# A four-stage graph network on one core: one-hots of the edge groups kept in DRAM, and the graph attention's work reordered

## What is computed

```python
h = relu(layernorm(x)); x = x + L0(h)     # weighted means over the edges, both directions
h = relu(layernorm(x)); x = x + L1(h)     # graph convolution, then 64 experts, top 2
h = relu(layernorm(x)); x = x + L2(h)     # 4 layers of attention by angle
h = relu(layernorm(x)); x = x + L3(h)     # 3 layers of graph attention, 4 heads

def _agnn_layer(h, src, dst, beta, n):    # L2, then relu
    h_norm = h * rsqrt(sum(h * h, -1, keepdims=True) + EPS)
    logits = beta * sum(h_norm[src] * h_norm[dst], -1)
    ex = exp(logits - segment_max(logits, dst, n)[dst])
    alpha = ex / (segment_sum(ex, dst, n)[dst] + EPS)
    return segment_sum(alpha[:, None] * h[src], dst, n)

def _gat_layer(x, src, dst, W, a_s, a_d, b):   # L3; every node below 1250 also has a loop
    h = (x @ W).reshape(n, 4, 64)
    e = leaky_relu(einsum(h, a_s)[src] + einsum(h, a_d)[dst], 0.2)
    ex = exp(e - segment_max(e, dst, n)[dst])
    alpha = ex / segment_sum(ex, dst, n)[dst]
    return segment_sum(h[src] * alpha[:, :, None], dst, n).reshape(n, 256) + b
```

## Time and profile before

| | |
|---|---|
| median of 3 runs | 11506.84 us (11502.91 to 11520.86) |
| span of the profiled execution | 10530.5 us, first to last instruction |
| the profiled execution's own time | not recorded apart; the median is 976.3 us above the span |
| mean granted TensorE clock | 0.835 of full speed |
| busy: PE, DVE, POOL, ACT | 6904.0, 5833.4, 5746.5, 2558.8 us |
| DMA | 825.78 MB, mean 78 GB/s |
| sort and first edge pass | up to about 220 us set-up, records to 1220 us, pass to 1957 us |
| attention by angle | 4472 to 7500 us |
| graph attention | 7612 to 10516 us |

### The profile page before, as it was taken

How to read it: one execution, slowest core, us unless ns; L and a number is a source line. 1 busy time by engine, 2 the same in 40 slices (tenths; PEclk the granted TensorE clock), 3 DMA queues, 4 the chain that set the end, 5 groups by cost and what they waited for, 6 DMA issues and landing times. The chain is left out here.

```text
span 10530.5 us, 156243 instructions
## 1 busy us (share of the span) xinstructions
PE 6904.0 (66%) x33524; PEld 5256.9 (50%) x33525; DVE 5833.4 (55%) x21353; ACT 2558.8 (24%) x6822; POOL 5746.5 (55%) x5970
## 2 busy tenths in 40 slices
PE   0000043333455579289799699699499989998997
PEld 0000033233244368178588588588356656665664
DVE  6000122322321311488788788788677768776887
ACT  0000000000000122122222222222155545554554
POOL 1777577676574021267477577477255535553553
PEclk9999999965676589699899899899767767777776
DMA  2000022424344079144544544544333333342333
GB/s 78 2 2 2 20 52 52 45 52 48 88 106 72 8 254 291 59 105 98 81 98 99 81 100 99 80 100 99 51 79 77 78 65 78 77 76 67 78 78 64
DMA packets 602104, 825.78 MB, mean 78 GB/s; under 512 B 297027, under 2 KB 423468, under 8 KB 602046
## 3 DMA queue, kind: packets, MB, share of 16 engines
q0 software_dynamic: 257472, 626.24, 29.4%
q1 hardware_dynamic: 344574, 198.99, 6.8%
HBM read 752.23 MB, written 72.83 MB: 78 GB/s over the span
## 5 line engine op out<-in xcount | busy, mean ns | idle before, releaser
L1258 POOL DMA_INDIRECT hs<-tab_agnn,rec x1984 | 1963.8, 990 | 1157.0 <-issue 594.3
L1692 POOL DMA_INDIRECT hs<-tab_gat,rec x1488 | 1406.6, 945 | 1294.5 <-DVE msg L1761 876.5
L511 PE MATMUL ps<-msg,oh 128*128 128x129 f32 x1984 | 510.5, 438 | 2040.8 <-DVE msg L486 2040.8
L511 PEld LDWEIGHTS ps<-msg,oh 128*128 128x128 f32 x1984 | 444.1, 329 | 2107.1 <-DVE oh L482 1229.3
L1868 PE MATMUL psV<-msg,ohf 128*128 128x260 f32 x2976 | 1279.6, 606 | 0.2 <-DVE msg L1761 0.2
L1730 DVE CUSTOM_DVE_ANT_0 cand<-psL,neg 128x512 f32<-128x512 f32 x1488 | 991.8, 686 | 258.0 <-issue 168.6
L1279 DVE CUSTOM_DVE_ANT_0 prod<-psG,hs 128x256 f32<-128x256 f32 x1984 | 841.9, 480 | 440.2 <-DMA hs<-tab_agnn,rec 359.9
L1868 PEld LDWEIGHTS psV<-msg,ohf 128*128 128x128 f32 x2976 | 902.1, 317 | 205.7 <-issue 1.5
L1408 PE MATMUL psV<-hs,pr 128*128 128x258 f32 x3968 | 998.2, 395 | 6.2 <-DVE pr L1318 6.2
L375 POOL DMA_INDIRECT rec_d<-slot x784 | 750.9, 958 | 425.3 <-DVE slot L356 235.0
L1384 PE MATMUL psG<-HN,ohT 128*128 x3968 | 969.7, 389 | 5.1 <-ACT neg L1353 5.1
(11 more groups left out here) (304 smaller groups left out, 12608.8 us busy)
## 6 DMA issues: line engine op xcount, KB each, us to landing
w<-in_L_gnn_w SPq DMA_DIRECT2D x224, 512.0 KB
hs<-tab_agnn,rec POOLq DMA_INDIRECT x1984
hs<-tab_gat,rec POOLq DMA_INDIRECT x1488
rec<-rec_d SPq DMA_DIRECT2D x1240, 8.0 KB
x<-xbuf SPq DMA_DIRECT2D x112, 128.0 KB, 4.1
ybuf<-y POOLq DMA_DIRECT2D x112, 128.0 KB, 4.3
tab_agnn<-H SPq DMA_DIRECT2D x4, 3250.0 KB, 11.4
xbuf<-acc SPq DMA_DIRECT2D x4, 3200.0 KB, 24.1
```

What stands on the lines that cost most here:

```text
L511: mm = nc.tensor.matmul(ps[:, j % 2, 0:cols], oh[:, j % 2, g, :], r, start=(g == 0), stop=(g == G - 1))
L1258: nc.gpsimd.indirect_dma_start(out=hs[:, j, g, :], out_offset=None, in_=k.tab_agnn, in_offset=bass.IndirectOffsetOnAxis(ap=rec[:, j, g, 0: ...
L1692: nc.gpsimd.indirect_dma_start(out=hs[:, j, g, :], out_offset=None, in_=k.tab_gat, in_offset=bass.IndirectOffsetOnAxis(ap=rec[:, j, g, 0:1 ...
```

## The change

1. The first edge pass (`sum_messages` with `keep=True`, key 0, by dst) keeps four buffers of one-hots, transposes each tile on PE, copies the transposes on ACT, and SP stores both to `oh_d` and `ohT_d` (124 x 128 x 512 float32 each). SP issues a group's stores four steps later and waits for all at the end.
2. Both attentions load them: `ohT` at lag 0, `oh` at lag 1, by SP. The making, transposing and copying of one-hots there goes.
3. Padding records point at row NP = 3200, and each table has 128 more rows, zeroed once; the two `below` minima go.
4. Graph attention: the two leaky steps become one over both parts, ACT copies `peak` and multiplies the messages of the fourth tile, DVE's message product (three tiles, one instruction) moves to the end of the step behind `acc`, and PE issues `psL` ahead of `psV`.
5. The semaphores of the two first stages are cleared and freed together, with a barrier.

```diff
 # sum_messages, keep
+        OR = U if keep else 2
+        oh = sb("oh", [P, OR, G, P], F32)
...
+                    if keep and (old := lagged(i, j, U)):
+                        _, _, t4 = old
+                        sp.dma_start(slab(k.oh_d, t4), oh[:, j, :, :].rearrange("p g e -> p (g e)")).then_inc(s_oh_kept[j], 16)
+                        sp.wait_ge(s_ohT, t4 + 1)
+                        sp.sem_inc(q.gate_sp, 1)
+                        sp.dma_start(slab(k.ohT_d, t4), ohT[:, j, :]).then_inc(s_ohT_kept[j], 16)
...
+                        for g in range(G):
+                            tr = nc.tensor.transpose(psT[:, j % 2, g * P:(g + 1) * P], oh[:, j, g, :], k.ident[:, :])
...
+                        nc.scalar.activation(ohT[:, j, :], psT[:, j % 2, :], ACT.Copy).then_inc(s_ohT, 1)
 # both attentions, SP (the angle's waits; graph attention waits q.v in place of s_p)
+                            if not (isinstance(i, int) and i == 0):
+                                sp.wait_ge(q.q, flow(t - U + 1))
+                            sp.dma_start(flat(ohT, j), slab(k.ohT_d, t)).then_inc(q.ld_ohT[j], 16)
+                        if last := lagged(i, j, 1):
+                            _, j1, t1 = last
+                            if not (isinstance(t1, int) and t1 < U):
+                                sp.wait_ge(s_p, own(t1 - U + 1))
+                            sp.dma_start(flat(oh, j1), slab(k.oh_d, t1)).then_inc(q.ld_oh[j1], 16)
 # attention by angle, DVE
-                            V.tensor_scalar(below[:, h3, :], tt[:, h3, :], 0.0, None, ALU.min).then_inc(q.min, 1)
-                            V.tensor_tensor(oh[:, j, :, :], mid(k.iota[:, :], G), b3(recf[:, j, :, 1], P),
-                                            ALU.is_equal).then_inc(q.oh, 1)
 # graph attention, DVE, behind the four maxima
+                                V.tensor_tensor(at_block(smax, b), at_block(smax, b), mt[:, h2, :], ALU.max).then_inc(s_mx, 1)
+                                V.tensor_tensor(raw[:, now, GH:], at_block(smax, b), at_block(sd, b), ALU.add).then_inc(s_mx, 1)
+                                V.scalar_tensor_tensor(out=leaky[:, now, part], in0=raw[:, now, part], scalar=NEG_SLOPE,
+                                                       in1=raw[:, now, part], op0=ALU.mult, op1=ALU.max).then_inc(s_leak, 1)
+                                V.tensor_tensor(df[:, h2, :], at_block(peak, b), leaky[:, now, GH:], ALU.subtract).then_inc(q.df, 1)
                             if add:
                                 dve.wait_ge(q.rs, flow(t4) + 1)
                                 dve.wait_ge(q.v, nth(t4) + 1)
...
+                            if old:
+                                dve.wait_ge(q.e, flow(t) + 1)
+                                V.tensor_tensor(hmsg[:, 0:GA, :, 0:C_HEAD], hrow[:, 0:GA, :, 0:C_HEAD],
+                                                hmsg[:, 0:GA, :, C_HEAD].unsqueeze(3).to_broadcast([P, GA, HEADS, C_HEAD]),
+                                                ALU.mult).then_inc(q.msg3, 1)
 # graph attention, ACT
+                                nc.scalar.activation(at_block(peak, b), leaky[:, j % 2, GH:], ACT.Copy).then_inc(q.m, 1)
...
+                                for m in range(HEADS):
+                                    lo = m * CH1
+                                    ins = nc.scalar.activation(msg[:, h, GA, lo:lo + C_HEAD], hs[:, j3, GA, lo:lo + C_HEAD], ACT.Copy,
+                                                               scale=msg[:, h, GA, lo + C_HEAD:lo + CH1])
```

More of the change, by code:

```diff
@@ L64, with __init__, __enter__, __call__ @@
     pass
+class Semaphores:
+    def __init__(self, nc):
+        self.nc, self.held = nc, []
+    def __enter__(self):
+        return self
+    def __call__(self, name):
+        self.held.append(self.nc.alloc_semaphore(tagged(self.nc, name)))
+        return self.held[-1]
+    def __exit__(self, *_):
+        self.nc.clear_and_free_semaphores(self.held)
+        self.nc.all_engine_barrier()
+        return False
 class Chain:
@@ L422, in _, with sum_messages @@
                     sp.wait_ge(q.ln_st, 16 * write(sp, q.ln_st))
-def sum_messages(nc, k, turn, key, table, width, weighted):
+def sum_messages(nc, k, turn, key, table, width, weighted, keep=False):
     cols = width + 1 if weighted else width
@@ L591, in _ @@
                 sp.wait_ge(s_rs, 2)
-                sp.dma_start(rows(k.tab_gc), k.acc[:, :, 0:D]).then_inc(s_st, 16)
+                sp.dma_start(rows(k.tab_gc[0:NP, :]), k.acc[:, :, 0:D]).then_inc(s_st, 16)
                 sp.wait_ge(s_st, 16)
@@ L1338, in step @@
                     def step(i, j):
-                        now, mid_, old = lagged(i, j, 0), lagged(i, j, 2), lagged(i, j, 3)
+                        last, mid_, old = lagged(i, j, 1), lagged(i, j, 2), lagged(i, j, 3)
                         if old:
@@ L1366, in step @@
                     def step(i, j):
-                        now, last, mid_, old = (lagged(i, j, n) for n in range(4))
+                        last, mid_, old = (lagged(i, j, n) for n in range(1, 4))
                         if mid_:
@@ L1751, in step @@
                             if old:
-                                dve.wait_ge(q.tt, flow(t) + 1)
-                                V.tensor_scalar(below[:, h, :], t3[:, h, :], 0.0, None, ALU.min).then_inc(q.min, 1)
+                                dve.wait_ge(s_leak, step_of(t + 1) + 1)
+                                V.tensor_tensor(g3(t3, h), g3(leaky, now), q3[:, :, 1, :], ALU.subtract).then_inc(q.tt, 1)
                             if mid_:
-                                dve.wait_ge(s_mx, own(t2) * 3 + 1)
@@ L1818, in step @@
[L1818 to L1831 removed]
+                                act.wait_ge(q.tt, flow(t) + 1)
@@ L1832, in step @@
+                                weights = msg[:, h, :, :].rearrange("p g (h c) -> p (g h) c", h=HEADS)[:, :, C_HEAD]
+                                nc.scalar.activation(weights, t3[:, h, 0:GH], ACT.Exp).then_inc(q.e, 1)
                             if mid_:
-                                _, j2, t2 = mid_
                                 act.wait_ge(q.df, flow(t2) + 1)
+                                if not (isinstance(t2, int) and t2 < 1):
+                                    act.wait_ge(q.q, flow(t2))
@@ L1840, in _ @@
+                        pipeline(act, step, 3, numbers=blocks)
                     @block.tensor
@@ L1876, in step @@
                                     nc.tensor.matmul(psL[:, m, :], sel[0:PARTS, m, :], sT[:, h1, :], start=True, stop=True).then_inc(q.b, 1)
+                            if add:
+                                i4, j4, t4 = add
+                                h4 = j4 % 2
+                                pe.wait_ge(s_msgA, own(t4) + 1)
+                                pe.wait_ge(q.msg3, own(t4) + 1)
+                                pe.wait_ge(q.ld_oh[j4], loaded(i4))
+                                if not (isinstance(t4, int) and t4 < 2):
+                                    pe.wait_ge(q.u, nth(t4 - 1))
+                                for g in range(G):
+                                    mm = nc.tensor.matmul(psV[:, h4, 0:W_GAT], oh[:, j4, g, :], msg[:, h4, g, :],
+                                                          start=(g == 0), stop=(g == G - 1))
+                                mm.then_inc(q.v, 1)
                             if mid_:
+                                pe.wait_ge(q.ld_ohT[j2], loaded(i2))
                                 pe.wait_ge(q.m, flow(t2) + 1)
```

313 lines of the change are left out of this document (150 added, 163 removed).

## The result

The changed kernel takes 12117.08 us (median of 4 runs, 12102.77 to 12124.58) where the kernel before takes 11504.88 (4 runs, 11496.9 to 11520.86) beside it: ratio 1.0532, interval 1.0512 to 1.0552. That is 612 us slower; the forecast was 597.

The account below looks back on a forecast made before the run. DVE was taken to bound graph attention, POOL's gathers attention by angle and the edge passes. Graph attention +588, attention by angle -16, first edge pass +25 gave +597 on 11506.84: 12104 us, range 11600 to 12320.

Parts of the forecast that it names:

- Graph attention, +588: Graph attention, three layers: psL issued before psV lengthens a step from 7.19 to 8.77 us, 196 us a layer.
- The bound of +759: Graph attention: upper bound if all of psV runs at the lower clock level, 3.66 us, giving a 9.23 us step.
- the ring: Graph attention: DVE's maxima release psL, then psV, then DVE's acc, message product and next maxima; 8.49 us, carried as 8.77.
- Attention by angle, -16: Attention by angle, four layers: -75 us from shorter gathers, +59 from loads at pass ends; bounds -75 to +42.
- only what POOL regains counts: Attention by angle: POOL is the bound, so removing DVE's one-hot gains only shorter gathers, 0.18 us per group.
- the price of the loads: Attention by angle: two loads add 0 to 1.62 us to each of 18 end groups; half taken, +59 for four layers.
- Rival 3: Attention by angle: loads make gathers land 1.62 us later throughout, step 5.46 to about 6; 12374 us, chance 0.08.
- Rival 4: Attention by angle: DVE's 32-bit pr instructions block POOL, step 6.2 instead of 5.46 us; 12418 us, chance 0.03.
- The two rows held against the Trainium skill's rule: Gathers: 0.42 us for one collision, at most 961 ns beside msg; held against blocking of up to 0.69 us per group.
- First edge pass, +25: First edge pass: stores cost nothing mid-pass, 0 to 29 us at the end, final waits and barrier 5 to 15.
- The 976 us outside the span: Whole kernel: median 11506.84 us against profiled span 10530.5; the 976.3 us difference taken as fixed, outside the span.
- Rivals 1 and 2: Graph attention: 1, psV at the upper clock, 11613 us, chance 0.12; 2, the ring does not close, 11251 us, chance 0.12.

Follow-up runs that it names:

- the kernel before's second profile: The kernel before, no edit, profiled once more on a chip of the faster kind: span 10520.1 us, median 10516.68 us over 8 runs.

## Why the prediction was right, and where it was not

**Graph attention, +588: right in mechanism, place and nearly in size.** Forecast was a step of 8.77 us with psV 0.5 us behind the fourth maximum and DVE idle for it by 2 us or more; measured 8.90, 0.6, and 3.16. A layer costs 1194.4 - 972.8 = 222 us more on the faster chips, 662 to the end of the kernel, against 196 and 588. The term most mis-sized is psV: taken as 3.2 us, it lasts 3.83 in the step shown, and its weight loads have a mean of 329 ns, above the 317 of the earlier trace rows; the granted clock was 0.60 in 8600 to 9300 us of the changed kernel, nearer to its lower level (0.5) than the 0.72 before. By itself that would have given 9.40. The step shown (9005.13 to 9013.97, 8.84) without psV is 5.01 and not 5.29, and it is 0.06 shorter than the steady mean where I had carried 0.28: +0.63, -0.28 and -0.22 make the 0.13 between 8.77 and 8.90. The bound of +759 was nearer than I placed it. Of the ring's cost 203 us a layer goes with the order alone (1194.4 - 991.7), and the loads take 19 (991.7 - 972.4), twice what two profiles of one code differ by; I had called them covered.

**Attention by angle, -16: wrong, +137.** The gain was counted as 0.18 us a group and is 0.16, but not by the reason given: with the compare alone gone from DVE, POOL regained its 0.18 and the step kept its length. The sentence "only what POOL regains counts" is therefore too simple; POOL also waits for psV to free its buffers. The step that failed is the price of the loads, counted at the ends only: I asked whether they fit into the free DMA share and not whether the gathers land later beside them. They cost 0.40 us in every full group, where I had none, and 0.83 at each end, where I had half of 1.62. Rival 3 had this mechanism, with the price too high (+270) and the chance at 0.08. Rival 4 didn't happen: gathers have a mean of 948 ns in the changed kernel. The two rows held against the Trainium skill's rule were misread. The collision of the earlier trace rows had 0.54 us of the compare left and cost 0.42, like the 31 above; and the 961 ns beside msg test nothing, since in 7700 to 8300 us of the kernel before's second profile only 2 of 336 gathers start while msg runs, both within 0.02 us of its start. What kept the gain small is that only 31 gathers of 73 groups meet the compare so.

**First edge pass, +25: small, as said, and less.** The tables' writes are 1435.8 us apart before (1270.4 to 2706.2, first two passes) and 1442.7 after (1271.4 to 2714.1): 7 us, less than the 15 by which the kernel before's two profiles differ (1421.2 and 1435.8). The bounds were 5 to 45.

**The 976 us outside the span: wrong.** They are the difference between a profile at one level of speed and times at the other. At the level of the result, before's stages were not profiled. The changed kernel is 793 us longer there than on the faster chips: 265 up to attention by angle, 511 in it (128 a layer), 17 in graph attention. The kernel before is about 990 longer. That the change costs 612 there and 827 elsewhere means that the kernel before loses some 200 us more on that chip than the changed one does. My guess at the place is graph attention, where the changed kernel has 3.16 us of idleness a step to lose such waits in and the kernel before has none; it was not tried, since no run fell on such a chip.

**So the sum was right by more than its reasons.** On the chips of the experiments 597 would have been 204 short of the profiles' 801 (graph attention 74, attention by angle 153, less 23 for the first pass); on the chip of the result 612 was met because something there hid about as much. That is luck: the number 12104 fits to 0.1%, but the -16 in it should have been about +137, and graph attention's +588 about +662. What was right is the mechanism of the ring and some nine tenths of its size.

**Rivals 1 and 2** fell as argued. The clock did not rise for psV, and the ring closed in 368 of 372 steps.

## What to carry to other kernels

On an engine that keeps its written order, the place of a long group of instructions relative to a wait can count for more than its length (here 620 and 728 us for one exchange): look for what is queued behind every wait, on both engines of the pair, and follow it round until it closes (or doesn't). Work taken off the bounding engine is worth what the next ring allows, which here was nothing at first (7.17 us a step with and without the lighter DVE), then 30 us a layer once two more orders were changed. Loading what could be computed isn't free because the mean DMA share has room: price it by what lands later beside it. And before a difference between span and time is taken as fixed, ask for the profiled execution's own time.

## What was unexpected of the hardware

The same program took 11,505 us in one set of runs and 10,496 to 10,514 on three chips in the others, the changed one 12,117 and 11,324. In the slower set DVE's `acc` in the second edge pass idles 9.6 us before 27 of 100 instructions with a releaser the trace doesn't resolve, and a layer of attention by angle takes 128 us more, while graph attention's steady steps wait the same for psV (246.8 us in 78 waits) and a layer of it takes 5 us more. Instruction fetches moved 0.39 MB in both profiles of the changed kernel, in 47 and 48 packets, so a larger amount of code loaded isn't what differs; the cause stays open.
